# First cross-attention of a four-layer kernel: context times projection weights made once, probabilities divided ahead of their transposition, tile loop written out

## The chip, the cores and the metric

The kernel runs on one core of a Trainium2 chip. The metric is the device time of one execution in microseconds, as the median of several. The program computes four transformer layers (a cross-attention and a feed-forward part each); the change touches the first cross-attention alone, a stretch of about 70 us near the start.

## The reference, cut to what matters

`c` is the layer-normalised input (2 batches of 1024 tokens of 256), `q` the context (2 batches of 64 tokens of 256). `W_l` has 4 blocks of 256 columns, one for each part of the concatenation.

```python
def _L0_xattn_ref(c, q, w_cq, b_cq, w_c, b_c, w_q, b_q, W_l, b_l):
    cq = jnp.einsum('bcd,bqd,d->bcq', c, q, w_cq) + b_cq
    s = (c @ w_c + b_c)[:, :, None] + (q @ w_q + b_q)[:, None, :] + cq
    a = jax.nn.softmax(s, axis=2)
    c2q_att = jnp.einsum('bcq,bqd->bcd', a, q)
    b_att = jax.nn.softmax(jnp.max(s, axis=2), axis=1)
    q2c_att = jnp.einsum('bc,bcd->bd', b_att, c)[:, None, :]
    x = jnp.concatenate([c, c2q_att, c * c2q_att, c * q2c_att], axis=-1)
    return x @ W_l.T + b_l
x = x + _L0_xattn_ref(_layernorm(x), ctx_1024, ...)
```

The stretch computes blocks two and three: u = a q, and u W2 + (c*u) W3. Blocks one and four need sums over all tokens and are made behind it.

## The kernel before, in words

The 2048 tokens are 16 tiles of 128; one turn of the loop takes the tiles `it` of both batches together, so there are 8 turns, called turn 0 to turn 7 below. The arguments of `step` are four tiles in a row: `step(one, two, three, four)` finishes tile `one`, while `two`, `three` and `four` are in earlier phases. `first` runs the early phases of tiles 0, 1 and 2 before turn 0. The order on each engine is the order in which the functions are called in `first` and `step`; engines meet through semaphores (`wait_ge` and `then_inc`), and nothing reorders.

The way of one tile: VectorE normalises it (`normal`, L682) - TensorE transposes it (`transposes`, L560) - ScalarE copies it to `cT` (L635) - TensorE makes scores: a bias (L566) and the product with the scaled context (L570) - VectorE takes row maxima (L688) - ScalarE takes the exponential into `a` and its sums (L641) - TensorE transposes `a` (L577), ScalarE copies it to `aT` (L648) - TensorE multiplies with the context (`mix`, L584) - VectorE divides by the sums and multiplies with c: `uv` (L695, L700, L703) - TensorE transposes `uv`, 8 blocks (L592), ScalarE copies them to `uvT` (L654) - TensorE projects with 8 products of 256 columns (`project`, L602) - VectorE adds to the residual `x_res` (L709). A float32 product that is no transposition stands in the trace as two matmuls, a transposition as one. GpSimd keeps copies of c and cT and adds the bias of the projection (L735 to L739).

The loop is made by `pipeline`: turns 0 to 4 are one hardware loop, turns 5, 6 and 7 stand behind it as loops of one turn each, without the calls whose tile is past the end. TensorE's order in a turn: `probs_transposed(two)`, `scores(three)`, `mix_transposed(one)`, `transposes(four)`, `mix(two)`, `project(one)`. VectorE's: `maxima(three)`, `normal(four)`, `mixed(two)`, `add(one)`.

Of the kernel before, what the change touches and what calls it, by code (L numbers as in the profile page):

```python
# [7 lines left out]
ALU = mybir.AluOpType  # L8
# [471 lines left out]
def l0_xattn(e, given, ffn):  # L480
# [3 lines left out]
    with ExitStack() as ctx:  # L484
# [11 lines left out]
        aT = sb("aT", [P, P])  # L496
        uv = sb("uv", [P, 2, 2, D])
        uvT = sb("uvT", [P, 2, 4, P])
# [11 lines left out]
        with nc.Block(no_gpsimd_drain=True) as block:  # L510
# [15 lines left out]
            def _(v):  # L526
# [13 lines left out]
                s.mix_ready, s.out_psum, s.x_done, s.bias_added)  # L540
        each = (s.probs_ready, s.mix_psum, s.mixT_psum, s.mixT_ready)
        begin(1, *both)
        begin(2, *each)
        C_BANK, SCORES, MIX, MIX_T, OUT, PROBS_T = 0, 1, 2, 4, 6, 7
        pair_of = lambda buf, it: buf.rearrange("p (b t) n -> p b t n", b=BATCH)[:, :, bass.ds(it, 1), :].rearrange("p b t n -> p b (t n)")
        with nc.Block(no_gpsimd_drain=True) as block:
# [7 lines left out]
            def _(pe):  # L554
# [19 lines left out]
                def probs_transposed(it):  # L574
                    pe.wait_ge(s.probs_ready.sem, s.probs_ready.at(it, 2))
                    pe.wait_ge(s.probsT_ready.sem, s.probsT_ready.before(it))
                    pe.transpose(ps[PROBS_T][:, 0:P], flat(a[:]), e.ident[:]).then_inc(s.probsT_psum.sem, 1)  # L577

                def mix(it):
                    pe.wait_ge(s.probsT_ready.sem, s.probsT_ready.at(it))  # L580
                    pe.wait_ge(s.mix_ready.sem, s.mix_ready.before(it))
                    for b in range(BATCH):
                        own = slice(b * CTX, (b + 1) * CTX)
                        pe.matmul(ps[MIX + b][:, 0:D], aT[own, :], e.ctx_tok[own, b, :], start=True, stop=True)\  # L584
                          .then_inc(s.mix_psum.sem, 1)

                def mix_transposed(it):
                    pe.wait_ge(s.mix_ready.sem, s.mix_ready.at(it))
                    for b in range(BATCH):
                        pe.wait_ge(s.mixT_ready.sem, s.mixT_ready.before(it, b + 1))  # L590
# [3 lines left out]
                        mm.then_inc(s.mixT_psum.sem, 1)  # L594

                def project(it):
                    pe.wait_ge(s.x_done.sem, s.x_done.before(it))
                    for b in range(BATCH):
                        pe.wait_ge(s.mixT_ready.sem, s.mixT_ready.at(it, b + 1))
                        own = slice(b * D, (b + 1) * D)  # L600
                        for k in range(4):
                            mm = pe.matmul(ps[OUT][:, own], uvT[:, b, k, :], w_l[:, 2 + k, :], start=(b, k) == (0, 0), stop=k == 3,  # L602
                                           skip_group_check=True)
                    mm.then_inc(s.out_psum.sem, 1)

                def first(one, two, three):
# [20 lines left out]
                turns_of_tiles(pe, e.chain["pe"], first, step, depth=4)  # L627

            @block.scalar
            def _(act_):  # L630
# [14 lines left out]
                def copy_aT(it):  # L645
                    act_.wait_ge(s.probsT_psum.sem, s.probsT_psum.at(it))
                    act_.wait_ge(s.mix_psum.sem, s.mix_psum.before(it, 2))
                    nc.scalar.copy(aT[:], ps[PROBS_T][:, 0:P]).then_inc(s.probsT_ready.sem, 1)  # L648

                def copy_uvT(it):  # L650
                    act_.wait_ge(s.out_psum.sem, s.out_psum.before(it))
                    for b in range(BATCH):
                        act_.wait_ge(s.mixT_psum.sem, s.mixT_psum.at(it, b + 1))
                        nc.scalar.copy(flat(uvT[:, b, :, :]), ps[MIX_T + b][:, :]).then_inc(s.mixT_ready.sem, 1)  # L654

                def first(one, two, three):
# [5 lines left out]
                    exp(two)  # L662

                def step(one, two, three, four):
                    if two is not None:
                        copy_aT(two)
                    copy_uvT(one)
# [5 lines left out]
                turns_of_tiles(act_, act, first, step, depth=4)  # L673

            @block.vector
            def _(v):
# [14 lines left out]

                def mixed(it):
                    v.wait_ge(s.probs_ready.sem, s.probs_ready.at(it, 2))
                    for b in range(BATCH):
# [2769 lines left out]
```

## Time and profile before

| | us |
|---|---|
| median of 3 runs | 1603.34 (1602.52 to 1605.77) |
| the profiled execution, its own time | 1602.76 |
| its span, first to last instruction | 1601.0 |
| first cross-attention's loop, first transposition to last addition | 22.5 to 90.6 |
| mean granted TensorE clock | 0.925 |

The span is the time between the first and the last instruction in the profile; 1.8 us of the execution's time lie outside it. In rows of the timeline the columns are: start in us from the span's beginning, length in us, engine, source line, operation, output<-inputs, count of instructions merged, and in brackets the idle time of the engine just before and what ended it. PEld is TensorE's weight load. The length of a merged matmul row ends with the modelled end of the last one, which overlaps the next row: the pace of TensorE is read from starts, not from lengths.

### The profile page before, as it was taken

The page shows a single profiled execution, that of the slowest core. Times are in us where ns is not written, and L with a number is a line of the kernel's source. Part 1 is how long each engine was busy: PE and PEld are TensorE (multiplying, and loading weights), DVE is VectorE, ACT ScalarE, POOL GpSimd, SP SyncE. Part 2 cuts the span into 40 slices and gives each one's busy share as a digit, 9 for nine tenths or more (in the row PEclk, how much of TensorE's full clock was granted, in tenths as well). Part 3 has the DMA queues.
Part 4 walks back from the last instruction along what each step waited for, and adds up shares of the span by engine and source line. Part 5 has one row for each costly group of instructions (what it writes and reads, how often), then busy time and mean ns, then how long its engine had stood idle before and what let it go on. Part 6 is the DMA issues. An engine that isn't in the chain of part 4 may idle for free. (4 is left out here: it accounts for less than half of the span.)

```text
span 1601.0 us, 29168 instructions
## 1 busy us (share of the span) xinstructions
PE 1356.9 (85%) x9286; PEld 1066.1 (67%) x9287; DVE 1019.5 (64%) x2724; ACT 763.4 (48%) x1822; POOL 536.6 (34%) x584
## 2 busy tenths in 40 slices
PE   4977999999999999999998797919945689739993
PEld 3855877877787778877876465716733357539993
DVE  3446776767677777777774754358968769662223
ACT  1323665556655665666565234126746456313331
POOL 3222222222222323232321206545642624225551
PEclk9988999999999999999999798959977589969997
DMA  8000000000000100000001444244010000102124
GB/s 312 21 1 1 1 1 1 0 1 0 0 27 2 36 1 0 0 0 0 0 1 34 182 197 142 89 154 172 1 41 1 3 4 2 53 24 68 65 66 168
DMA packets 29278, 74.94 MB, mean 47 GB/s; under 512 B 7800, under 2 KB 13193, under 8 KB 27389
## 3 DMA queue, kind: packets, MB, share of 16 engines
q1 hardware_dynamic: 22364, 55.63, 9.3%
q0 software_dynamic: 6816, 18.14, 3.6%
q8 instruction: 46, 0.75, 0.2%
q14 instruction: 52, 0.42, 0.1%
HBM read 54.41 MB, written 20.88 MB: 47 GB/s over the span
## 5 line engine op out<-in xcount | busy, mean ns | idle before, releaser
L1107 PE MATMUL banks<-l_ffn_in_wqkv,l_ffn_hT 128*128 128x512 f32 x384 | 178.3, 600 | 0.0
L1190 PE MATMUL banks<-l_ffn_h2T,l_ffn_in_w 128*128 128x128 f32 x1408 | 175.7, 277 | 0.0
L1190 PEld LDWEIGHTS banks<-l_ffn_h2T,l_ffn_in_w 128*128 128x128 f32 x1408 | 167.0, 192 | 7.3 <-issue 5.7
L1319 ACT ACTIVATE l_ffn_work<-l_ffn_work,l_ffn_att_bias 128x256 f32<-128x256 f32 x256 | 126.4, 495 | 70.6 <-DVE l_ffn_att_bias L1475 70.6
L1348 ACT ACTIVATE l_ffn_gate<-banks,l_ffn_layer_cols 128x128 f32<-128x128 f32 x160 | 51.7, 364 | 183.5 <-PE banks L1190 170.2
L1041 POOL TENSOR_TENSOR l_ffn_rden_wide<-l_ffn_att_rden,ones 128x512 f32<-128x512 f32 x32 | 33.2, 1039 | 251.0 <-DVE l_ffn_att_rden L1486 251.0
L1107 PEld LDWEIGHTS banks<-l_ffn_in_wqkv,l_ffn_hT 128*128 128x128 f32 x384 | 68.1, 190 | 71.7 <-issue 71.6
L1198 PE MATMUL banks<-l_ffn_in_w,l_ffn_ff 128*128 128x256 f32 (+1 forms) x384 | 104.5, 388 | 0.0
L2981 POOL TENSOR_TENSOR L__probs<-L__probs,L__rec 128x1024 f32<-128x1024 f32 x32 | 60.9, 1902 | 100.5 <-DVE L__rec L2941 100.5
L1046 POOL TENSOR_TENSOR l_ffn_rstd<-l_ffn_ve,neg_half 128x1 f32<-128x1 f32 x32 | 20.0, 625 | 208.6 <-DVE l_ffn_ve L1512 208.6
L1356 ACT ACT_TABLE_LOAD x68 | 87.2, 1283 | 1.2
L2435 PEld LDWEIGHTS banks<-l_experts_rowT,l_plan_c_all 128*128 128x128 f32 x624 | 77.5, 196 | 1.9
L2435 PE MATMUL banks<-l_experts_rowT,l_plan_c_all 128*128 128x128 f32 x624 | 77.6, 279 | 0.0
L1130 PE MATMUL banks<-l_ffn_in_kT,l_ffn_qT 64*128 64x256 f32 x512 | 75.4, 392 | 2.3 <-ACT l_ffn_qT L1313 2.3
L1031 POOL TENSOR_TENSOR l_ffn_rn<-l_ffn_ss,neg_half 128x8 f32<-128x8 f32 x32 | 52.6, 1643 | 70.6 <-DVE l_ffn_ss L1427 70.6
L1139 PEld LDWEIGHTS banks<-ident,l_ffn_work 128*128 128x128 f32 x512 | 57.4, 141 | 27.7 <-issue 14.8
L1528 DVE SCALAR_TENSOR_TENSOR l_ffn_ff<-banks,l_ffn_layer_cols,l_ffn_gate 128x128 f32<-128x128 f32 x192 | 58.1, 344 | 26.1 <-ACT l_ffn_gate L1348 21.3
L2444 PE MATMUL banks<-l_ffn_in_w,l_experts_upT 128*128 x312 | 73.6, 379 | 0.0
L1198 PEld LDWEIGHTS banks<-l_ffn_in_w,l_ffn_ff 128*128 128x128 f32 (+1 forms) x384 | 63.0, 190 | 14.5 <-issue 10.6
L1139 PE MATMUL banks<-ident,l_ffn_work 128*128 128x128 f32 x512 | 64.5, 275 | 6.8 <-ACT l_ffn_work L1319 6.8
L1481 DVE COPY l_ffn_pT<-banks 128x512 f32<-128x512 f32 x64 | 42.6, 666 | 35.1 <-PE banks L1139 35.1
L1155 PE MATMUL banks<-l_ffn_pT,l_ffn_in_vv 128*64 128x128 f32 x1024 | 63.0, 276 | 0.0
(444 smaller groups left out, 3348.7 us busy)
## 6 DMA issues: line engine op xcount, KB each, us to landing
l_plan_rows<-l_plan_pairs SPq DMA_DIRECT2D x16, 512.0 KB, 8.0
l_ffn_in_w<-in_L_w SPq DMA_DIRECT2D x2, 4096.0 KB, 17.5
l_ffn_in_down<-in_L_down SPq DMA_DIRECT2D x1, 4096.0 KB, 13.6
l_plan_pairs<-l_plan_rows SPq DMA_DIRECT2D x4, 1024.0 KB, 7.0
l_plan_table<-l_plan_rows SPq DMA_DIRECT2D x8, 512.0 KB, 2.7
l_ffn_in_wqkv<-in_L_wqkv SPq DMA_DIRECT2D x1, 3072.0 KB, 12.0
l_ffn_in_w<-in_L_w SPq DMA_DIRECT2D x4, 640.0 KB, 12.3
x_res<-in_x SPq DMA_DIRECT2D x4, 512.0 KB, 5.3
```

The lines of the kernel that those rows point to most:

```text
L1107: mm = pe.matmul(ps[:, (Q, K, V)[n], :], hT[:, m.b, m.odd, ch, 1 - ch:P + 1 - ch], wqkv[:, bass.ds(m.layer, 1), ch, n * INNER:(n + 1) * IN ...
L1130: mm = pe.matmul(ps[:, SCORES + 2 * g + n, half * 2 * P:(half + 1) * 2 * P], qT[own, m.b, j, :], flat(kT[own, m.b, j, :, :]), start=True, ...
L1139: mm = pe.transpose(ps[:, SCORES + j, n * P:(n + 1) * P], work[:, m.b, 2 * j + n // 2, (n % 2) * P:(n % 2 + 1) * P], e.ident[:])
L1155: mm = pe.matmul(ps[n * DH:(n + 1) * DH, MIXED, j * P:(j + 1) * P], vv[:, m.b, c, h * DH:(h + 1) * DH], pT[:, m.b, 2 * slot_of(h) + c, :], ...
L1190: mm = pe.matmul(ps[:, HIDDEN[pair], to:to + P], w1[:, ch, at:at + P], h2T[:, ch, m.b, :], start=(j % 2, n, ch) == (0, 0, 0), stop=ch == D ...
L1198: mm = pe.matmul(ps[:, DOWN, 0:D], ff[units(j), j, :], w2[units(j), bass.ds(m.layer, 1), j, :].rearrange("p l n -> p (l n)"), start=j == 0 ...
L1319: ex = nc.scalar.activation(work[:, m.b, slot, :], work[:, m.b, slot, :], ACT.Exp, bias=bias[:, m.b, slot:slot + 1], scale=-1.0, accum_out ...
L1356: act.link(nc.scalar.activation(unused[:], zero, func))
L1528: ins = v.scalar_tensor_tensor(ff[own, j, :], ps[own, HIDDEN[pair], of:of + P], cols[own, col:col + 1], gate[own, j, :], ALU.add, ALU.mult)
L2435: mm = pe.matmul(ps[m.j][:, f * P:(f + 1) * P], up_w[:, m.j, at:at + P], rowT[:, m.j, ch, :], start=(f, ch) == (0, 0), stop=ch == DCH - 1, ...
L2444: mm = pe.matmul(ps[3 + m.j][:, 0:D], upT[:, m.j, f, :], down_weight(x, f), start=f == 0, stop=f == MCH - 1)
L2981: p.tensor_tensor(probs[:, m.b, :, :], probs[:, m.b, :, :], rec[:, m.b, :].unsqueeze(2).broadcast_to((P, XH, CTX)), ALU.mult)\
```

## The change

The projection of u is folded: u W2 = a (q W2). `ctx_w` = q W2 is made once (`folded`, four matmuls in the trace) and copied by ScalarE. Per tile, `project` takes `aT` times `ctx_w` (64 rows of the array for each batch) and only c*u goes the long way, over 4 transpositions instead of 8 and 4 products instead of 8. So that `a` is divided before it is transposed, VectorE does `divide` (a reciprocal and a product of 128x128) between the exponential and the transposition of `a`; `mixed` is then one product that reads PSUM. `aT` has two buffers, since the projection reads it a turn later. The output of the projection takes two PSUM banks, the transposed product one. The loops of TensorE, ScalarE and VectorE are written out in Python; GpSimd's remains. TensorE's order in a turn has `scores(three)` ahead of `probs_transposed(two)`; VectorE's begins with `divide(two)`.

```diff
@@ TensorE
 def probs_transposed(it):
-    pe.wait_ge(s.probs_ready.sem, s.probs_ready.at(it, 2))
+    pe.wait_ge(s.scaled.sem, s.scaled.at(it))
+def folded():
+    for ch in range(DCH):
+        mm = pe.matmul(ps[MIX_T][:, 0:D], e.ctxT[:, ch, :, :], w_l[:, 2 + ch, :], start=ch == 0, stop=ch == DCH - 1)
+    mm.then_inc(s.kT_ready.sem, 1)
 def mix_transposed(it):
     for b in range(BATCH):
-        for k in range(4):
-            mm = pe.transpose(ps[MIX_T + b][:, k * P:(k + 1) * P],
-                              uv[:, b, k // 2, (k % 2) * P:(k % 2 + 1) * P], e.ident[:])
+        for ch in range(DCH):
+            k = b * DCH + ch
+            mm = pe.transpose(ps[MIX_T][:, k * P:(k + 1) * P], cu[:, b, ch * P:(ch + 1) * P], e.ident[:])
 def project(it):
     pe.wait_ge(s.x_done.sem, s.x_done.before(it))
     for b in range(BATCH):
-        own = slice(b * D, (b + 1) * D)
-        for k in range(4):
-            mm = pe.matmul(ps[OUT][:, own], uvT[:, b, k, :], w_l[:, 2 + k, :], start=(b, k) == (0, 0), stop=k == 3,
+        own = slice(b * CTX, (b + 1) * CTX)
+        pe.matmul(ps[OUT + b][:, 0:D], aT[own, it % 2, :], ctx_w[own, :], start=True, stop=False)
+    pe.wait_ge(s.mixT_ready.sem, s.mixT_ready.at(it))
+    for b in range(BATCH):
+        for ch in range(DCH):
+            mm = pe.matmul(ps[OUT + b][:, 0:D], cuT[:, b * DCH + ch, :], w_l[:, 4 + ch, :], start=False, stop=ch == DCH - 1)
 def first(one, two, three):
     ...
     mix(one)
+    folded()
+    pe.wait_ge(s.kT_ready.sem, s.kT_ready.at(0, 2))
 def step(one, two, three, four):
+    if three is not None:
+        scores(three)
     if two is not None:
         probs_transposed(two)
-    if three is not None:
-        scores(three)
@@ ScalarE
 def copy_aT(it):
-    act_.wait_ge(s.mix_psum.sem, s.mix_psum.before(it, 2))
+    if it >= 2:
+        act_.wait_ge(s.out_psum.sem, s.out_psum.at(it - 2))
+def copy_ctx_w():
+    act_.wait_ge(s.kT_ready.sem, s.kT_ready.at(0))
+    nc.scalar.copy(ctx_w[:], ps[MIX_T][:, 0:D]).then_inc(s.kT_ready.sem, 1)
@@ VectorE
+def divide(it):
+    v.wait_ge(s.probs_ready.sem, s.probs_ready.at(it, 2))
+    dve.link(v.reciprocal(a_rec..., a_sum...[:, :, it:it + 1]))
+    v.tensor_tensor(a[:], a[:], a_rec[:].unsqueeze(2).broadcast_to((P, BATCH, CTX)), ALU.mult).then_inc(s.scaled.sem, 1)
 def mixed(it):
-    (two reciprocals, two products u = PSUM * a_rec, one product of both batches with c)
+    v.tensor_tensor(cu[:], e.psum[:, MIX:MIX + BATCH, 0:D], pair_of(c_all[:], it)..., ALU.mult).then_inc(s.mix_ready.sem, 1)
 def first(one, two, three):
     normal(one)
     normal(two)
     maxima(one)
+    divide(one)
     normal(three)
     maxima(two)
     mixed(one)
 def step(one, two, three, four):
+    if two is not None:
+        divide(two)
     if three is not None:
         maxima(three)
```

The order on TensorE in turn 5 before (turns 0 to 4 have besides the transpositions L560 x4 ahead of L584). L577 is the transposition of `a`, L566 and L570 the scores, L592 the transpositions of `uv`, L584 the mix, L602 the projection:

```order
L577 MATMUL banks<-ident,l_xattn_a 128x128
L566 MATMUL banks<-l_xattn_q_bias,ones 128x128
L570 MATMUL banks<-l_xattn_qcat,cT 128x64 x4
L592 MATMUL banks<-ident,l_xattn_uv 128x128 x8
L584 MATMUL banks<-ctx_tok,l_xattn_aT 128x256 x2
L602 MATMUL banks<-l_xattn_in_w_l,l_xattn_uvT 128x256 x8
```

And TensorE in a turn of the change that still has all its calls (turns 0 to 4):

```order
L576 MATMUL banks<-l_xattn_q_bias,ones 128x128
L580 MATMUL banks<-l_xattn_qcat,cT 128x64 x4
L587 MATMUL banks<-ident,l_xattn_a 128x128
L608 MATMUL banks<-ident,l_xattn_cu 128x128 x4
L570 MATMUL banks<-ident,c_tile 128x128 x4
L599 MATMUL banks<-ctx_tok,l_xattn_aT 128x256 x2
L615 MATMUL banks<-l_xattn_ctx_w,l_xattn_aT 128x256 x2
L619 MATMUL banks<-l_xattn_in_w_l,l_xattn_cuT 128x256 x4
```

The scores moved ahead of the transposition of `a`; four transpositions and four whole products went, two half-height products came, right behind the two of the mix.

VectorE in turn 5 before (maxima, reciprocals, u, c*u, addition):

```order
L688 TENSOR_REDUCE l_xattn_nmax<-banks 128x2
L695 RECIPROCAL l_xattn_a_rec<-l_xattn_a_sum 128x1 x2
L700 TENSOR_SCALAR l_xattn_uv<-banks,l_xattn_a_rec 128x256 x2
L703 TENSOR_TENSOR l_xattn_uv<-l_xattn_uv,l_xattn_c_all 128x2x256
L709 TENSOR_TENSOR x_res<-banks,x_res 128x2x256
```

And of the change:

```order
L717 RECIPROCAL l_xattn_a_rec<-l_xattn_a_sum 128x2
L718 TENSOR_TENSOR l_xattn_a<-l_xattn_a,l_xattn_a_rec 128x128
L711 TENSOR_REDUCE l_xattn_nmax<-banks 128x2
L724 TENSOR_TENSOR l_xattn_cu<-banks,l_xattn_c_all 128x512
L731 TENSOR_TENSOR x_res<-banks,x_res 128x2x256
```

The reciprocal went ahead of the maxima with a product behind it, right after the addition of the turn before; of the three products between maxima and addition one is left.

## Rows read from the trace of the kernel before

**Rows 1.** Windows: busy time of each engine, granted clock (PEclk), DMA share, GB/s.
```profile
22.00:26.00 4.00, 2.83 (x12) 2.43 (x13) 2.02 (x4) 1.02 (x2) 3.05 (x5) 1.00 1.05 428
28.80:32.20 3.40, 3.39 (x17) 3.06 (x17) 0.42 (x3) 0.27 (x1) 1.89 (x3) 1.00 0.93 393
50.86:58.27 7.41, 6.99 (x44) 5.79 (x43) 3.42 (x9) 2.53 (x8) 2.39 (x3) 1.00 0.00 0
118.00:120.00 2.00, 1.29 (x6) 0.78 (x5) 1.97 (x4) 1.95 (x4) 0.37 (x1) 1.00 0.00 0
```

**Rows 2.** Timeline of turn 3 with the start of turn 4, all engines.
```profile
58.27 0.27 PE L577 MATMUL banks<-ident,l_xattn_a 128*128 128x128 f32 x1
58.58 0.69 DVE L709 TENSOR_TENSOR x_res<-banks,x_res 128x512 f32 x1 [1.97 <-PE banks L602]
58.60 1.00 PE L570 MATMUL banks<-l_xattn_qcat,cT 128*128 128x64 f32 x8
58.67 0.27 ACT L648 COPY l_xattn_aT<-banks 128x128 f32<-128x128 f32 x1 [3.17 <-PE banks L577]
59.44 1.04 PE L592 MATMUL banks<-ident,l_xattn_uv 128*128 128x128 f32 x8
59.75 0.29 DVE L688 TENSOR_REDUCE l_xattn_nmax<-banks 128x128 f32 x1 [0.48 <-PE banks L570]
60.11 0.74 DVE L682 TENSOR_SCALAR c_tile<-x_res,mean_var,rstd 128x256 f32 x2
60.91 0.66 PE L560 MATMUL banks<-ident,c_tile 128*128 128x128 f32 x4 [0.42 <-DVE c_tile L682]
61.49 0.70 PE L584 MATMUL banks<-ctx_tok,l_xattn_aT 64*128 64x256 f32 x4
62.12 3.72 PE L602 MATMUL banks<-l_xattn_in_w_l,l_xattn_uvT 128*128 128x256 f32 x16
65.47 0.14 PEld L577 LDWEIGHTS banks<-ident,l_xattn_a 128*128 128x128 f32 x1
65.68 0.27 PE L577 MATMUL banks<-ident,l_xattn_a 128*128 128x128 f32 x1
```

**Rows 3.** Timeline of the last turns, 5 to 7.
```profile
73.09 0.27 PE L577 MATMUL banks<-ident,l_xattn_a 128*128 128x128 f32 x1
79.53 0.27 PE L577 MATMUL banks<-ident,l_xattn_a 128*128 128x128 f32 x1
84.80 1.04 PE L592 MATMUL banks<-ident,l_xattn_uv 128*128 128x128 f32 x8
86.22 3.69 PE L602 MATMUL banks<-l_xattn_in_w_l,l_xattn_uvT 128*128 128x256 f32 x16 [0.39 <-ACT l_xattn_uvT L654]
```

**Rows 4.** Timeline of `first` and of turn 0.
```profile
28.81 0.47 PE L577 MATMUL banks<-ident,l_xattn_a 128*128 128x128 f32 x1 [1.28 <-ACT l_xattn_a L641]
33.52 0.47 PE L577 MATMUL banks<-ident,l_xattn_a 128*128 128x128 f32 x1 [0.20 <-ACT l_xattn_a L641]
34.32 1.81 PE L570 MATMUL banks<-l_xattn_qcat,cT 128*128 128x64 f32 x8
37.63 1.06 PE L560 MATMUL banks<-ident,c_tile 128*128 128x128 f32 x4
38.62 1.23 PE L584 MATMUL banks<-ctx_tok,l_xattn_aT 64*128 64x256 f32 x4
39.78 3.83 PE L602 MATMUL banks<-l_xattn_in_w_l,l_xattn_uvT 128*128 128x256 f32 x16
```

**Rows 5.** Groups by line, shapes kept apart, VectorE.
```profile
L2029 DVE TENSOR_TENSOR l_route_equal<-l_route_equal,l_route_expert_number 128x128 f32<-128x128 f32 x4 | 1.2, 292 | 0.1
L695 DVE RECIPROCAL l_xattn_a_rec<-l_xattn_a_sum 128x1 f32 x10 | 1.1, 151 | 0.0
L703 DVE TENSOR_TENSOR l_xattn_uv<-l_xattn_uv,l_xattn_c_all 128x512 f32<-128x512 f32 x8 | 5.5, 692 | 1.3 <-DVE l_xattn_uv L700 1.1
```

**Rows 6.** Waits from 20 to 92 us (total, times, longest); one timeline row of ScalarE.
```profile
DVE l_xattn_uv L703 <- DVE l_xattn_uv L700: 1.1, 5, 0.2
109.22 0.37 ACT L1296 COPY l_ffn_hT<-banks 128x256 f32<-128x256 f32 x1
```

More of the change, by code:

```diff
@@ L495, in l0_xattn @@
         a_rec = sb("a_rec", [P, 2])
-        aT = sb("aT", [P, P])
-        uv = sb("uv", [P, 2, 2, D])
-        uvT = sb("uvT", [P, 2, 4, P])
+        aT = sb("aT", [P, 2, P])
+        ctx_w = sb("ctx_w", [P, D])
+        cu = sb("cu", [P, BATCH, D])
+        cuT = sb("cuT", [P, BATCH * DCH, P])
         top = sb("top", [P, BATCH])
@@ L539, in l0_xattn, with unrolled @@
         both = (s.c_kept, s.cT_kept, s.c_ready, s.cT_psum, s.cT_ready, s.scores_psum, s.max_ready, s.probsT_psum, s.probsT_ready,
-                s.mix_ready, s.out_psum, s.x_done, s.bias_added)
-        each = (s.probs_ready, s.mix_psum, s.mixT_psum, s.mixT_ready)
+                s.mix_ready, s.out_psum, s.x_done, s.bias_added, s.mixT_psum, s.mixT_ready, s.scaled)
+        each = (s.probs_ready, s.mix_psum)
+        begin(2, s.kT_ready)
         begin(1, *both)
         begin(2, *each)
-        C_BANK, SCORES, MIX, MIX_T, OUT, PROBS_T = 0, 1, 2, 4, 6, 7
+        C_BANK, SCORES, MIX, MIX_T, OUT, PROBS_T = 0, 1, 2, 4, 5, 7
+        def unrolled(engine, order, first, step):
+            order.begin(engine)
+            each_tile = [*range(TILES), None, None, None]
+            first(*each_tile[0:3])
+            for n in range(TILES):
+                step(*each_tile[n:n + 4])
         pair_of = lambda buf, it: buf.rearrange("p (b t) n -> p b t n", b=BATCH)[:, :, bass.ds(it, 1), :].rearrange("p b t n -> p b (t n)")
@@ L583, in mix @@
                         own = slice(b * CTX, (b + 1) * CTX)
-                        pe.matmul(ps[MIX + b][:, 0:D], aT[own, :], e.ctx_tok[own, b, :], start=True, stop=True)\
+                        pe.matmul(ps[MIX + b][:, 0:D], aT[own, it % 2, :], e.ctx_tok[own, b, :], start=True, stop=True)\
                           .then_inc(s.mix_psum.sem, 1)
@@ L625, in step @@
                     project(one)
-                turns_of_tiles(pe, e.chain["pe"], first, step, depth=4)
+                unrolled(pe, e.chain["pe"], first, step)
             @block.scalar
@@ L662, in first @@
                     exp(two)
+                    copy_ctx_w()
                 def step(one, two, three, four):
@@ L666, in step @@
                         copy_aT(two)
-                    copy_uvT(one)
+                    copy_cuT(one)
                     if four is not None:
@@ L671, in step @@
                         exp(three)
-                turns_of_tiles(act_, act, first, step, depth=4)
+                unrolled(act_, act, first, step)
             @block.vector
@@ L727, in step @@
                     add(one)
-                turns_of_tiles(v, dve, first, step, depth=4)
+                unrolled(v, dve, first, step)
             @block.gpsimd
@@ L740, in l0_xattn @@
         end(TILES, *both, *each)
+        end(1, s.kT_ready)
         s.max_ready.each(2)
```

32 lines of the change are left out of this document (12 added, 20 removed).

## The prediction

> **What bounds the kernel now.** I read the windows first, then the timeline. TensorE is busy 6.99 of the 7.41 us of turn 2, VectorE 3.42 and ScalarE 2.53 [rows 1]: in a steady turn TensorE has the work, and what it waits for is VectorE. The timeline of turn 3 [rows 2] shows how, counted from its first matmul at 58.27. The transposition of `a` and the scores run until 1.17, the 8 transpositions of `uv` (L592) from 1.17 to about 2.1; then 0.42 us of idle (0.65 by its weight loads) until the normalised tile is there at 2.64 (60.91), because VectorE may take the maxima (1.48) only after the scores and normalises behind that. Transpositions and the mix take to 3.85 (62.12), the projection 3.56 to 7.41 (65.68). So the projection is almost half of the turn, and each of its 16 matmuls is worth about 0.21 us (the weight loads run from 62.12 to 65.47, 3.35 us for 16). Turn 5 takes 6.44, turn 6 5.27, turn 7 4.98 us up to the end of its projection (86.22 + 16 x 0.222 = 89.78) [rows 3]. In `first` and the early part of turn 0 TensorE is at half its later pace: 4 transpositions and what follows take 0.99 us at 37.63 and 0.58 at 60.91, the mix 1.16 at 38.62 and 0.63 at 61.49; from 39.78 on the pace is the later one (16 matmuls in 3.67) [rows 2, 4]. That is the lower clock level, 1.2 GHz, until about 40 us and 2.4 GHz behind it, though the column of the granted clock reads 1.00 in both [rows 1].
>
> **The steady turns (1 to 4), part by part.** Again from the first matmul behind the last projection.
> - VectorE: the addition starts at 0.31 and ends at 1.00 as now [rows 2]. Then comes `divide`: a reciprocal of 0.15 and a product of 128x128 in SBUF, 0.29 (L2029, same shape, also with a broadcast operand) [rows 5]. With 0.03 between instructions it ends at 1.50. Between an instruction and one that waits for it the trace has more in one place: 1.1 us in 5 waits ahead of L703, 0.22 each [rows 6]; that would give 1.70. I take 1.50, since L703 waits for a reader of PSUM and the reciprocal reads SBUF.
> - TensorE: scores from 0 to 1.06 (moved ahead, they hide two thirds of the wait for `divide`), idle until 1.55, `a` transposed, 4 transpositions of `cu` to 2.1. Maxima 1.53 to 1.82 and the normalised tile at 2.61: transpositions at 2.68 against 2.64 now. So the 4 transpositions saved (0.44) buy nothing: they turn into the idle time ahead of L587. Mix at 3.27.
> - Projection: four half-height matmuls behind the four of the mix. Four halves now take 0.63 from 61.49 to 62.12 [rows 2] where four whole ones take 0.85; two groups are 1.26 at most, and 1.07 if the pairs follow without a break (4 x 0.2135 + 0.2). I take 1.26. Then 8 whole matmuls, 1.71. End 6.24 against 7.41: **1.17 us a turn, 4.7 for four turns**. Bounds: 1.17 - 0.20 (the longer link) = 0.97, and 1.17 + 0.19 = 1.36.
> - Hidden: `copy_aT` (1.95 to 2.22), `copy_cuT` (2.4 to 3.0, one copy instead of two), `mixed` (one product of 0.69 [rows 5], from about 4.0) end before TensorE asks for them. Behind `divide` on VectorE wait the maxima, the next tile and `mixed`; their delay is the 0.04 above. GpSimd needs 2.39 us a turn [rows 1]. Should `copy_cuT` come late its price is at most the 0.6 that it takes.
>
> The Trainium skill, "TensorEngine Tiling (Array Packing)", section Theoretical Speedup, promises up to twice the rate for a contraction of at most 64 rows. The rows show 0.63 for four halves where that rule says 0.43. By the rule the eight halves would be 0.85 instead of 1.26 and the whole sum 0.4 x 7 = 3 us larger; I go by the row.
>
> Against the change speaks the Trainium skill, "VectorE: DVE Perf Modes", section on the TRN2 errata: a fixed latency is exposed by every instruction, so that small ones cost mostly that. The product of 128x128 at 0.292 against 0.692 for four times the elements [rows 5] agrees. Its formula of 58 cycles plus one per element gives 0.19, and 0.1 us a turn less; the trace's 0.29 stands.
>
> **The last turns.** Turn 5 has no next tile. `a` transposed at 1.55, its copy done 2.22 (ScalarE starts 0.40 behind the matmul, 58.67 - 58.27 [rows 2], and takes 0.27), mix and halves 2.27 to 3.53, 1.71 more: 5.24 against 6.44, gain 1.2. Turn 6 has no scores, so nothing covers `divide` any more: again 5.24, against 5.27, gain 0. Turn 7: 4 transpositions, the halves wait for the addition (1.06), 0.63, 1.71: 3.40 against 4.98, gain 1.6. **Together 2.8**, so 7.5 us with the steady ones.
>
> **The front.** `divide(0)` puts the first transposition of `a` 0.54 later (28.81 [rows 4]: recip, product, hand-over), and nothing covers it, as everything behind it waits. `folded` adds 4 matmuls of 256 columns at the low level, 0.43 each, twice the 0.2135: 1.7. Then TensorE waits for ScalarE's copy of `ctx_w`: hand-over 0.4, copy of 256 columns 0.37 [rows 6], 0.75 in all. The wait for the exponential (0.20) goes. So turn 0 begins at 36.3 instead of 33.52. Up to its transpositions 4.11 us pass now (37.63); then the scores 2.13 (twice 1.06) and the chain of maxima, normalisation and hand-overs, 1.47 from the scores' end (59.44 to 60.91 [rows 2]), 3.60: transpositions at 39.9 against 37.63, 2.3 late. What remains of turn 0 is 5.82 us now (to 43.45: the projection's start 39.78 and 3.67). In the change it is 0.59 + 1.26 + 1.71 = 3.56 at the high level and twice, about 6.8, at the low one. With the rise at 40 us as before turn 0 ends at 43.5, no change; with all of it low at 46.7, 3.2 late. I take 0.5 late, near the first: TensorE is nearly as dense from 29 to 40 us as now, where it is busy 3.39 of 3.40 [rows 1]. **Front: +0.5 (-1.2 to +3.2).** The lower bound is a rise some 3 us earlier, by the dense matmuls of `folded`.
>
> **The loop written out** I cost at nothing: behind the taken branch at the end of turn 3 the next weight load starts at 65.47, right where the last one of the projection ends (62.12 + 3.35), and the short pauses ahead of the mix and the projection double in turn 0 [rows 2, 4], so they follow the array's clock, not register arithmetic. If the branches did hide something on another engine, it is under TensorE's work.
>
> **Sum.** -7.5 + 0.5 = -7.0 against the profiled execution's own 1602.76 (span 1601.0 and 1.8 around it): 1595.8. The median of the runs shown is 0.6 above that execution, so I expect 1596.4. Everything behind the stretch only shifts.
>
> **The rivals.**
> - *The clock rises a turn's length later and the links cost 0.2.* -7.5 + 6 x 0.2 + 3.2 = -3.1: 1602.8 - 3.1 + 0.6 = 1600.3. For it: the front has three new pauses (0.54, 0.75, 0.3 us), and now it takes until 40 us for TensorE to get the high level after a start with holes (busy 2.83 of 4 us at 22) [rows 1]. Against: these pauses are short beside those at 22 to 29.
> - *More gain:* the halves follow at full overlap (7 x 0.19 = 1.3) and the clock rises early (1.7 more): 1596.4 - 3.0 = 1593.4. For it: `folded` is 1.7 us of unbroken whole matmuls.
> - *Slower: the level stays low through the stretch.* A steady turn then is 2 x (1.06 + 0.11 + 0.44 + 0.59 + 1.26 + 1.71) = 10.3 us of TensorE work, against 7.41: +2.9 in each of four, +2.7, +1.8 and +0.6 in turns 5 to 7, +3.2 in turn 0: +20, 1623. It decides once the rise is 20 us late: each turn at the low level costs 10.3 - 6.24 = 4.1, and two of them eat the gain. For it: TensorE's idle share in a turn rises from 6% to 17%. Against: at the low level it would have no idle time at all, and a stretch with TensorE busy 1.29 of 2 us keeps the high level now [rows 1].
> - *The change does not shorten the path:* if VectorE were the engine that bounds the turn. Its 3.42 us of 7.41 fall (two products of 256 columns go, one of 128 comes); it is a partner in the chain, not the bound. Price at most 0.44 a turn (the halves of L592, already given up), so this has no case of its own.
>
> **How the numbers follow.** Forecast 0.60 (own range 1594.5 to 1599), late clock 0.17, more gain 0.12, slower by the clock 0.04, something behind the stretch that shifts with it 0.07, half of it to either side. 0.2% (3.2 us) is about what a measurement of this kernel tells from no change; faster is below 1600.1: 0.60 + 0.12 + a quarter of the late clock + 0.02 = 0.77; within 0.15; slower 0.08. The range 1593.5 to 1601.5 leaves out the slow case and the outer part of the early clock.
>
> **What would show it.** In the changed profile: four steady turns of 6.0 to 6.4 us between matmuls of L576; an idle of about 0.5 ahead of L587, released by VectorE's L718; transpositions L570 released by the normalised tile; 1.1 to 1.3 us from L599 to L619; turn 7 of about 3.4; a pause of about 0.75 ahead of the third scores; the double pace of the mix and projection from 40 to 43 us. Wrong would make it: turns of over 7 us, matmuls of turn 1 at the low pace, or another length of what follows the last addition.

## The result, and the profile after

The changed kernel took 1591.69 us (median of 6 runs, 1589.65 to 1593.3), the kernel before 1602.59 (6 runs, 1598.47 to 1605.77): ratio 0.9929 [0.9915, 0.9943], 10.9 us less. The forecast was 1596.4 with a range from 1593.5. The direction was right and the gain half as large again as forecast, so that the time lies below the range. The profiled execution took 1591.43 (span 1589.6) against 1602.76 (1601.0).

Windows of the changed kernel: core, columns and the first two stretches as in [rows 1], the third one is its turn 2.

```profile
22.00:26.00 4.00, 3.21 (x14) 2.81 (x15) 1.64 (x3) 0.95 (x2) 3.42 (x5) 1.00 1.05 392
28.80:32.20 3.40, 3.24 (x15) 2.96 (x15) 1.05 (x4) 0.27 (x1) 1.84 (x2) 1.00 0.92 393
47.36:53.09 5.73, 5.47 (x36) 4.35 (x35) 2.65 (x7) 2.04 (x7) 2.39 (x3) 1.00 0.01 1
```

A turn takes 5.73 us where it took 7.41, and TensorE is busy 5.47 of it where it was busy 6.99: of the 1.68 us that went, 1.52 are work that it no longer has and 0.16 idle time. The timeline of turn 2 of the changed kernel (start, duration, engine, line, idle time before and its releaser) answers to [rows 2]:

```profile
47.36 0.39 PE L576 MATMUL banks<-l_xattn_q_bias,ones 128*128 128x128 f32 x2
47.56 0.69 DVE L731 TENSOR_TENSOR x_res<-banks,x_res 128x512 f32<-128x512 f32 x1 [1.57 <-PE banks L619]
48.17 0.16 DVE L717 RECIPROCAL l_xattn_a_rec<-l_xattn_a_sum 128x2 f32<-128x2 f32 x1
48.36 0.29 DVE L718 TENSOR_TENSOR l_xattn_a<-l_xattn_a,l_xattn_a_rec 128x128 f32<-128x128 f32 x1
48.62 0.29 DVE L711 TENSOR_REDUCE l_xattn_nmax<-banks 128x2 f32<-128x128 f32 x1
48.70 0.14 PEld L587 LDWEIGHTS banks<-ident,l_xattn_a 128*128 128x128 f32 x1 [0.26 <-DVE l_xattn_a L718]
48.71 0.33 PE L587 MATMUL banks<-ident,l_xattn_a 128*128 128x128 f32 x1
48.83 0.73 DVE L705 TENSOR_SCALAR c_tile<-x_res,mean_var,rstd 128x256 f32<-128x256 f32 x2
49.61 0.42 PEld L570 LDWEIGHTS banks<-ident,c_tile 128*128 128x128 f32 x4 [0.38 <-DVE c_tile L705]
50.20 0.70 PE L599 MATMUL banks<-ctx_tok,l_xattn_aT 64*128 64x256 f32 x4
50.73 0.60 PE L615 MATMUL banks<-l_xattn_ctx_w,l_xattn_aT 64*128 64x256 f32 x4
51.26 1.99 PE L619 MATMUL banks<-l_xattn_in_w_l,l_xattn_cuT 128*128 128x256 f32 x8
53.09 0.38 PE L576 MATMUL banks<-l_xattn_q_bias,ones 128*128 128x128 f32 x2
```

From L576 on: `a` is transposed 1.35 later (forecast 1.55), `c` 2.25 (2.68), the mix comes at 2.84 (3.27), the mix and the halves take 1.06 (1.26), the whole products 1.83 (1.71). Ahead of its weight loads TensorE idles 0.26 us for `divide` and 0.38 for the normalised tile; before, it idled 0.65 for the tile alone:

```profile
60.90 0.42 PEld L560 LDWEIGHTS banks<-ident,c_tile 128*128 128x128 f32 x4 [0.65 <-DVE c_tile L682]
```

On VectorE the addition starts 0.20 behind the turn's first matmul, 0.31 before, and the normalisation 0.21 behind the start of the maxima, 0.36 before [rows 2]: a first hint at what the forecast left out.

The front of the changed kernel answers to [rows 4]:

```profile
28.96 0.48 PE L587 MATMUL banks<-ident,l_xattn_a 128*128 128x128 f32 x1 [1.80 <-DVE l_xattn_a L718]
33.41 1.92 PE L591 MATMUL banks<-l_xattn_in_w_l,ctxT 128*128 128x256 f32 x4
35.78 0.49 PE L576 MATMUL banks<-l_xattn_q_bias,ones 128*128 128x128 f32 x2 [0.46 <-ACT l_xattn_ctx_w L671]
36.11 1.00 PE L580 MATMUL banks<-l_xattn_qcat,cT 128*128 128x64 f32 x8
39.80 1.99 PE L619 MATMUL banks<-l_xattn_in_w_l,l_xattn_cuT 128*128 128x256 f32 x8
```

The eight scores at 36.11 take 1.00, the same eight before took 1.81 at 34.32 [rows 4]: TensorE is at its higher level, 2.4 GHz, from about 35 us instead of 40. The column of the granted clock shows 1.00 on both sides of the rise, so the durations have to be read.

The last turns answer to [rows 3]. Turn 6 waits for `divide` (1.19), turn 7 for the addition (0.35):

```profile
70.84 0.33 PE L587 MATMUL banks<-ident,l_xattn_a 128*128 128x128 f32 x1 [1.19 <-DVE l_xattn_a L718]
75.38 0.70 PE L615 MATMUL banks<-l_xattn_ctx_w,l_xattn_aT 64*128 64x256 f32 x4 [0.35 <-DVE x_res L731]
78.05 0.69 DVE L731 TENSOR_TENSOR x_res<-banks,x_res 128x512 f32<-128x512 f32 x1 [2.72 <-PE banks L619]
```

A clean measure of the stretch is the start of VectorE's last addition of each turn (turn 0, turn 1, ..., turn 7, us; before L709, after L731), read from each kernel's timeline:

| kernel | 0 | 4 | 5 | 6 | 7 | steady turn |
|---|---|---|---|---|---|---|
| before | 43.76 | 73.40 | 79.73 | 85.00 | 89.95 | 7.41 |
| changed | 41.83 | 64.76 | 69.70 | 74.64 | 78.05 | 5.73 |

The last addition is 11.90 us earlier, of which the span keeps 11.4. By part: turn 0 ends 1.93 earlier, turns 1 to 4 give 6.71, turn 5 gives 1.39, turn 6 0.33, turn 7 1.54.

### The profile page after: what moved, and what is told of

Read it like the earlier page. It is cut to its first block and busy times, and to the rows that moved or that the text cites. A ratio compares the mean times of both kernels' runs of the same rounds, so it can differ in the third digit from the quotient of the medians.

```text
span 1589.6 us, 28758 instructions
## 1 busy us (share of the span) xinstructions
PE 1345.3 (85%) x9226; PEld 1054.7 (66%) x9227; DVE 1013.2 (64%) x2708; ACT 758.7 (48%) x1815; POOL 534.3 (34%) x584
## 2 busy tenths in 40 slices
DMA packets 29278, 74.96 MB, mean 47 GB/s; under 512 B 7799, under 2 KB 13192, under 8 KB 27388
```

## The experiments

Three groups of runs, each beside runs of the kernel before: group 1 is the first four kernels, group 2 the next four, group 3 the last four. The kernel before took 1591.43 in group 1 (17 runs), 1601.88 in group 2 (11), 1603.14 in group 3 (23); in group 1 the times are some 11 us shorter, in the profiles of its four kernels in a later part with the experts' DMA transfers (102 us against 112 to 114 from the first row of the routing, `l_route_equal`, to the first addition of the experts' rows to `x_res`). So only ratios, and stretches within a profile, are compared across groups. Additions are given as in the table above.

**The loops of the kernel before, written out.** The arithmetic stays that of the kernel before.

```diff
-turns_of_tiles(v, dve, first, step, depth=4)        # and the same for pe and act_
+unrolled(v, dve, first, step)
```

> The kernel before with the three loops of TensorE, ScalarE and VectorE written out and nothing else. Theory A (the writing out takes register instructions off VectorE's part of the chain): the first normalised tile 0.3 to 0.5 us earlier, and 0.15 us between the maxima and the normalisation in each of turns 0 to 4, so a steady turn of 7.25 instead of 7.41; in all -1.2 us, about 1601.4 against 1602.6, ratio 0.999. Theory B (my prediction's: it costs and brings nothing): turn 7.41, ratio 1.000. Theory C (the loops hid most of what I missed): -3 us or more, turn 7.1 or less. The clock's rise should stay near 40 us under A and B, since TensorE's work is the same.

Additions 42.72 (turn 0), 71.28, 77.62, 82.89, 87.84: a steady turn takes 7.14 instead of 7.41, the last addition is 2.11 earlier. The four steady turns give 1.08 of that; the other 1.04 is turn 0, in whose front the first tile came 0.5 earlier (21.20) and the clock rose at about 38.5 us instead of 40. Three rows of VectorE in it, maxima, normalisation and addition:

```profile
57.00 0.69 DVE L717 TENSOR_TENSOR x_res<-banks,x_res 128x512 f32<-128x512 f32 x1 [1.92 <-PE banks L610]
58.17 0.29 DVE L696 TENSOR_REDUCE l_xattn_nmax<-banks 128x2 f32<-128x128 f32 x1 [0.48 <-PE banks L578]
58.38 0.73 DVE L690 TENSOR_SCALAR c_tile<-x_res,mean_var,rstd 128x256 f32<-128x256 f32 x2
```

From maxima to normalisation it is 0.21, as in the changed kernel. But the whole kernel is slower: 1597.19, ratio 1.0051 [1.0034, 1.0067]. From the start of the last addition to the first row of the routing (`l_route_equal`, at 940.7) it takes 852.9 us where it took 846.5, in the kernel before (936.5 - 89.95) and in the changed one (924.6 - 78.05). The loss is outside the stretch; the two experiments below that repeat and pad this kernel find most of it.

**The change with VectorE's loop as a hardware loop again.** All else is the change.

```diff
-unrolled(v, dve, first, step)
+turns_of_tiles(v, dve, first, step, depth=4)
```

> The changed kernel with VectorE's loop as a hardware loop again (TensorE and ScalarE stay written out). Theory A: the steady turn gets longer by 0.15 to 0.35 (5.9 to 6.1 instead of 5.73), the start 0.4 later: +1.2 to +2.2 us, 1593 to 1594. Theory B (VectorE's shorter hand-overs come from the changed order and not from the loop): turn 5.73, no change. The clock rises at the same place in the work.

1583.41, ratio 0.9961 [0.9948, 0.9974]. Additions 45.75, 69.75, 74.68, 79.62, 83.03: a steady turn of 5.99, 0.26 more than the change. The first normalised tile comes at 21.69 instead of 21.19. VectorE in a steady turn whose first matmul starts at 51.47:

```profile
51.78 0.69 DVE L731 TENSOR_TENSOR x_res<-banks,x_res 128x512 f32 x1 [1.47 <-PE banks L619]
52.84 0.29 DVE L711 TENSOR_REDUCE l_xattn_nmax<-banks 128x128 f32 x1
53.19 0.74 DVE L705 TENSOR_SCALAR c_tile<-x_res,mean_var,rstd 128x256 f32 x2
```

0.35 again from the maxima to the normalisation, and 0.31 from the matmul to the addition: 0.14 and 0.11 more than in the change (0.21 and 0.20), which together is the 0.26 of the turn, to a hundredth. Taken off the kernel before, with the other two, and put back on the changed one, VectorE's loop is worth 0.26 to 0.27 us a steady turn. TensorE's and ScalarE's loops, which stay written out here, bring nothing more that shows. The first tile is 0.5 later in both kernels with the loop, but also in a written-out one (21.77, the padded kernel below), so the 0.5 cannot be put down to the loop alone.

**The folded product made in the block before.** `folded` and its copy leave the path between turns.

```diff
 @@ block that makes kT, TensorE
+for ch in range(DCH): mm = pe.matmul(ps[4][:, 0:D], e.ctxT[:, ch, :, :], w_l[:, 2 + ch, :], ...)
 @@ first
-folded()
-pe.wait_ge(s.kT_ready.sem, s.kT_ready.at(0, 2))
```

> The changed kernel with the product of context and weights and its copy made in the block before the loop, so that TensorE's sequence in the front has neither the four matmuls nor the pause behind them. Theory D (the whole matmuls of the product bring the clock's rise forward from 40 to 35 us): without them in the loop's front the rise comes at 38 us or later, turn 0 is run at the low level, and the 2.4 us saved there are given back: between -0.5 and +1.5 us. Rival E (the rise comes at about 35 us whatever stands there, or by chance of its phase): -1.0 to -2.4 us, 1589.5 to 1590.7, with the transpositions of turn 0 already at the high level.

1580.32, ratio 0.9944 [0.993, 0.9957]. The third scores start at 34.41 instead of 35.78, though the first normalised tile comes 1.67 later (22.86 instead of 21.19; the copy of `ctx_w` and the products stand ahead of it). But TensorE reached the higher level only at about 39.1, and the additions (42.16, 65.09, 70.03, 74.96, 78.37) are not earlier than the change's. A gain of 1.4 was hidden by a clock that rose 4 us later.

**The normalisation of the tile four turns on, ahead of the addition.**

```diff
-if four is not None: normal(four)     # between maxima and mixed
 if two is not None: mixed(two)
+if one + 4 < TILES: normal(one + 4)
 add(one)
```

> The changed kernel with the normalisation of the next tile moved ahead of the addition, one turn earlier, so that it is done under the projection. Theory F (a steady turn is set by the chain addition, divide, maxima, normalisation, transposition): the transpositions of the next tile no longer wait, 0.35 us less in each of turns 0 to 4, turn 5.4: -1.7 us, 1590. Rival G (TensorE's own work or ScalarE's copies set the turn): no change, 5.7.

1578.72, ratio 0.993 [0.991, 0.995]. Additions 41.28, 63.35, 68.29, 73.23, 76.64: a steady turn of 5.52, and the last addition 1.41 ahead of the change's. TensorE's rows:

```profile
42.58 0.33 PE L587 MATMUL banks<-ident,l_xattn_a 128*128 128x128 f32 x1 [0.27 <-DVE l_xattn_a L718]
43.18 0.60 PE L570 MATMUL banks<-ident,c_tile 128*128 128x128 f32 x4
46.60 0.38 PE L576 MATMUL banks<-l_xattn_q_bias,ones 128*128 128x128 f32 x2
```

The wait ahead of L570 is gone; the one for `divide` is all that is left in a turn. In the time of the whole kernel the 1.41 us do not show: the ratio, 0.993, is that of the change (0.9929), and behind the last addition this profile takes 848.7 us up to the routing instead of 846.5.

**The change a second time**, unaltered, for what the clock does by itself.

> The changed kernel once more, unaltered, timed beside the kernel before on one chip, with a second profile. What it tells apart: whether the rise of TensorE's clock in the front, at about 35.1 us in the first profile of the change and at 40.0 in that of the kernel before, belongs to the kernel or to the execution. Theory H (chance of the execution: the written-out, the half-written-out and the folded-ahead variants rose at 38.5, 43.3 and 39.1): another moment than 35, anywhere from 35 to 43, turn 0 then ends between 41.8 and 45, everything from turn 1 on shifts by that. Rival D (the whole matmuls of the folded product bring it): 35 to 36 again. The time against before on one chip: stage 11.9 us shorter in the profile, 10 to 12 with the clock's chance, ratio 0.992 to 0.994.

1592.44, ratio 0.994 [0.9924, 0.9957]; its profiled execution took 1598.88. Its front:

```profile
33.43 2.07 PE L591 MATMUL banks<-l_xattn_in_w_l,ctxT 128*128 128x256 f32 x4
36.55 1.81 PE L580 MATMUL banks<-l_xattn_qcat,cT 128*128 128x64 f32 x8
42.44 2.16 PE L619 MATMUL banks<-l_xattn_in_w_l,l_xattn_cuT 128*128 128x256 f32 x8
```

The same eight scores take 1.81 instead of 1.00; the higher level comes at about 42.5, 7 us later than in the first profile of the same kernel. Turn 0 ends with the addition at 44.64 instead of 41.83; all later turns are equal to 0.01 (5.73; last addition 80.86). So 2.8 us between the two profiles are the moment of the rise alone. The last addition is 9.1 ahead of the 89.95 before in this profile and 11.9 in the first; neither of the two rose at the 40 us of the kernel before, where the gain would lie in between (an estimate: a rise 2.5 us earlier than in the second profile spares half of that, 1.25, so about 10.3). Another 4.7 of the 7.5 us between the two profiles lie behind the stretch: 851.2 us from the last addition to the routing against 846.5, of the same program. Counted by ScalarE's table loads, 2.5 of them fall in the first 77 us behind the last addition and 1.4 in the last 66 ahead of the routing; I have no cause for them. This profiled execution was also the slowest of its six, whose median is 1592.44. `folded` stood at the same place in both, so its dense matmuls do not by themselves bring an early rise. In the six profiles that have `folded` there, the halved durations of TensorE's rows begin at 35 to 36 us in three and at 42.5 to 44 in three; in the eight without it they begin between 37 and 40.

**Both edits together**: the folded product in the block before, and the normalisation ahead.

> The changed kernel with both: the folded product in the block before the loop, and the normalisation of the next tile ahead of the addition. If their effects add: turns of 5.52 and the front 2.4 us shorter less 1.3 for the longer block before, that is 2.3 us less than the change at the same moment of the clock's rise, 1.0 to 4 us with its chance; ratio to before 0.990 to 0.993. If the clock's rise gives the front's part back: 1.0.

1589.93 (7 runs), ratio 0.9923 [0.9907, 0.9938]: the lowest ratio here, 2.5 us under the change in the same group, but the intervals overlap, so that it is faster than the change is not shown. A steady turn takes 5.52 again; the last addition is at 78.11 with a rise at about 40, against 80.86 with 42.5.

**Old order on TensorE**, the scores behind the transposition of `a`.

```diff
-if three is not None: scores(three)
 if two is not None: probs_transposed(two)
+if three is not None: scores(three)
```

> The changed kernel with the order of before in one place: the transposition of the divided probabilities ahead of the next tile's scores. Theory (the move of the scores is what hides the division): TensorE idles about 1.3 us at the start of each steady turn, the scores come after it, and maxima and normalisation behind them; the transpositions of the next tile 3.7 us into the turn instead of 2.25: turn 7.1 instead of 5.73, about +7 us over turns 0 to 4, so nearly all the steady gain gone. Rival (the chain on VectorE is short enough to be hidden anyhow): turn below 6.2.

1603.39 (one run), additions 45.29, 74.32, 80.33, 85.27, 88.68: a turn of 7.26. TensorE in it:

```profile
53.69 0.33 PE L587 MATMUL banks<-ident,l_xattn_a 128*128 128x128 f32 x1 [1.18 <-DVE l_xattn_a L718]
56.12 0.66 PE L570 MATMUL banks<-ident,c_tile 128*128 128x128 f32 x4 [0.59 <-DVE c_tile L705]
```

`divide` uncovered is 1.18 of idle time, and the maxima and the normalisation behind the scores come late too: 1.53 us a turn, nearly all of the change's gain. With `divide` in the chain, the gain hangs on the order of two calls.

**The half-height products apart**, one batch after the other.

```diff
+pe.wait_ge(s.mixT_ready.sem, s.mixT_ready.at(it))
 for b in range(BATCH):
     pe.matmul(ps[OUT + b][:, 0:D], aT[own, it % 2, :], ctx_w[own, :], start=True, stop=False)
-pe.wait_ge(s.mixT_ready.sem, s.mixT_ready.at(it))
-for b in range(BATCH):
     for ch in range(DCH): ...
```

> The changed kernel with the same eight half-height matmuls of mix and projection, but those of the projection no longer in a row: batch 0's half product, its whole ones, batch 1's half product, its whole ones. Theory (the halves are cheap because pairs on different rows of the array run at the same time, 0.27 us a pair in a row): from the first mix matmul to the next turn 3.2 to 3.35 us instead of 2.90, turn 6.0 to 6.2. Rival (a half-height matmul is cheap by itself): 2.90, turn 5.73.

1598.23 (one run), a turn of 6.55, 0.82 more than the change:

```profile
45.45 0.70 PE L599 MATMUL banks<-ctx_tok,l_xattn_aT 64*128 64x256 f32 x4
45.98 0.59 PE L616 MATMUL banks<-l_xattn_ctx_w,l_xattn_aT 64*128 64x256 f32 x2
46.51 1.13 PE L618 MATMUL banks<-l_xattn_in_w_l,l_xattn_cuT 128*128 128x256 f32 x4
47.57 0.70 PE L616 MATMUL banks<-l_xattn_ctx_w,l_xattn_aT 64*128 64x256 f32 x2
48.19 1.13 PE L618 MATMUL banks<-l_xattn_in_w_l,l_xattn_cuT 128*128 128x256 f32 x4
49.16 0.38 PE L576 MATMUL banks<-l_xattn_q_bias,ones 128*128 128x128 f32 x2
```

From the mix to the next turn 3.71 us pass, in the change 2.90. A pair of records of L616 takes 0.53 and 0.62 here, where four take 0.53 in the change: alone, a half-height product costs more than a whole one of the change, where eight records take 1.83, a pair 0.46. The whole products between them take 0.20 more as well. In turns 5 to 7, where the halves now also wait for the copy of `cu` (0.19, 0.19 and 0.82 us), the loss is 1.24 to 1.27.

**The written-out kernel before, again**, unaltered.

> The kernel before with its three loops written out, once more. Its first profile was 2.1 us shorter in the stretch itself (turn 7.14 instead of 7.41, first tile 0.5 earlier), but 6 us longer in the feed-forward loop behind it, where VectorE waited 5.2 us ahead of one line (the scale of the attention, twice, about 100 us apart) instead of 3.0 without waiting for anything that the profile shows, and TensorE's clock fell to the low level twice behind it. Theory I (the written-out code moves VectorE's later loop to other places of its instruction stream, and instructions come late there): the same again, 5 us waits, ratio 1.003 to 1.006. Rival (chance of the execution): waits of 3.0 us, ratio about 0.9985.

1608.37 (12 runs), ratio 1.004 [1.0024, 1.0056]; the turn is 7.14 again, and from the last addition to the routing 855.1. In the first feed-forward part VectorE stands ahead of the same instruction, with nothing that the profile shows to wait for. The row of the kernel before, then of the first written-out run, then of this one:

```profile
251.00 0.28 DVE L1460 TENSOR_SCALAR l_ffn_att_scale<-l_ffn_rn 128x2 f32<-128x2 f32 x2 [2.91 <-issue]
```

```profile
248.55 0.29 DVE L1468 TENSOR_SCALAR l_ffn_att_scale<-l_ffn_rn 128x2 f32<-128x2 f32 x2 [5.18 <-issue]
```

```profile
250.29 0.29 DVE L1468 TENSOR_SCALAR l_ffn_att_scale<-l_ffn_rn 128x2 f32<-128x2 f32 x2 [5.11 <-issue]
```

And the windows of this run around it (columns as in [rows 1]):

```profile
250.00:255.00 5.00, 2.42 (x10) 1.89 (x11) 4.33 (x22) 3.57 (x15) 0.00 (x0) 0.71 0.01 2
255.00:260.00 5.00, 5.00 (x18) 2.77 (x18) 4.07 (x7) 2.75 (x6) 1.67 (x2) 0.61 0.00 0
```

TensorE runs dry behind that pause, and the granted clock falls to 0.71 and 0.61, where it is 1.00 in the kernel before. What the pauses cost can be read from the starts of ScalarE's table loads (`ACT_TABLE_LOAD`), of which the feed-forward loop has the same ones in every kernel. Between two of them, in us, in an undisturbed turn 13.3; "padded" is the next experiment:

| from (start in the kernel before) | before | written out | written out, again | padded |
|---|---|---|---|---|
| 244.24 | 15.5 | 19.4 | 19.4 | 13.3 |
| 336.66 | 15.7 | 18.9 | 19.0 | 13.3 |
| 611.33 | 14.4 | 14.4 | 14.4 | 16.9 |
| 702.59 | 14.4 | 14.4 | 14.4 | 18.2 |

The first two rows hold the pauses: about 3.0 us in the kernel before and 5.0 to 5.2 in the written-out one. They are 7.2 us of the loss, the same in both runs. The last 66 us ahead of the routing add 1.5 to 1.7, and the first 77 behind the last addition took 2.6 us less in the first run and 0.1 less in this one. Over all profiles the piece from the last addition to the routing takes 851.8 to 856.9 us in the four kernels with the old projection written out, and 845.8 to 851.2 in the ten others, the unaltered change with both 846.5 and 851.2 among them. So one profile's sum says little about it; the 7.2 us at two places in both runs, the means, 854.2 and 847.9, and the ratios of 12 and 6 runs say that the loss goes with this code. The changed kernel, written out as well, has pauses of 3.1 and 2.8 us there, like the kernel before; nothing in the edit was meant to bring that, so it is luck.

**The same, with 24 small instructions more on VectorE** ahead of the stretch, to move all later code of VectorE.

```diff
+for n in range(24):
+    v.memset(uv[:, 1, 1, n:n + 1], 0.0)
```

> The same with 24 instructions more on VectorE (memsets of one column each) in the block before, where VectorE waits for a load and they are hidden; they only shift where its later code lies. Theory I: the waits of 5.2 us change, to 3.0 as in the kernel before or to another length, and the time with them: 1 to 6 us less than the unpadded one, ratio 0.997 to 1.002. Rival (the place of the code does not matter): as the unpadded one within 1 us, waits 5.2.

The pause moved: 0.40 instead of 5.1 at this place, and 3.15 and 3.11 came up at the same line at 616 and 710 us, where no other kernel has one of over 2 us; ahead of one row of `oT` it is 5.5, as in two variants of the change, 3.3 in the kernel before. The time did not move: 1609.89 (12 runs), ratio 1.0036 [1.0022, 1.005], 856.9 us from the last addition to the routing.

```profile
250.12 0.28 DVE L1470 TENSOR_SCALAR l_ffn_att_scale<-l_ffn_rn 128x2 f32<-128x2 f32 x2 [0.40 <-issue]
```

So these pauses depend on where the code lies. Without padding they are the bulk of the loss (7.2 us by the table above); with it, compared with the kernel before, 4.6 us are gained at these two places and 6.3 lost at the two later ones, and the 5.5 ahead of `oT` costs 1.7. The padded kernel also takes 3.4 us more in the first 77 us and 3.1 more in the last 66. Why the place of the code makes VectorE pause is not shown, and neither is what makes up the rest. The first normalised tile comes at 21.77 here, as late as in the kernel before (21.70), though all three loops are written out.

**The division moved, no fold**: loops written out, `divide` and the scores as in the change, the projection as before.

```diff
+divide(two)      # and scores(three) ahead of probs_transposed(two)
-u = v.tensor_scalar(uv[:, b, 0, :], ps[MIX + b][:, 0:D], a_rec[:, b:b + 1], None, ALU.mult)
+u = v.tensor_copy(uv[:, b, 0, :], ps[MIX + b][:, 0:D])
```

> The kernel before with loops written out, the division ahead of the transposition and the scores ahead of it, but without the folded product: 8 transpositions and 8 whole products as before (u is copied out of PSUM undivided). Theory (the gain of a steady turn comes from the projection, the move of the division neither costs nor gains as long as the scores hide it): turn 7.1 to 7.25, against 7.14 without the division's move. Rival (the shorter chain on VectorE behind the mix is what gains): turn below 6.9.

1608.19 (one run), additions 43.17, 71.59, 78.26, 84.92, 89.87. The steady turn is 7.10 against 7.14 without the division: moved and covered, it is free in the steady turns. Turn 5, which has scores but no next tile, takes 6.67 instead of 6.34, and turn 6, without scores, 6.66 instead of 5.27: uncovered it costs 1.4. All of the gain of a steady turn beyond the loop is then the fold: 7.10 to 5.73.

**The kernel before, again.**

> The kernel before, unaltered, a second profile. Theory H (the moment of the clock's rise is the execution's chance): steady turns of 7.41 and the same waits on VectorE (3.0 in the feed-forward part), but turn 0 ends anywhere between 41 and 46 us instead of 43.45. Rival: 43.4 to 43.5 again.

1598.58 (one run); turn 7.41, additions 43.53, 73.17, 79.50, 84.77, 89.72, rise at about 39.9. Here the clock rose where it did in the first profile, 40.0. That it can vary by 7 us, as in the changed kernel, was not seen in these two; the two profiles of the written-out kernel before differ by about 1.5 (rise at 38.5 and 37, turn 0's addition at 42.72 and 41.99).

## Why the prediction fell short, step by step

- **Steady turns** (forecast 1.17 each, measured 1.68). The mechanism was right: the fold takes work off TensorE, the scores cover `divide`, the four transpositions saved (0.44) turn for the most part into idle time. By its weight loads TensorE idles 0.65 us in a turn before and 0.90 in the change with VectorE's loop put back; in the change itself it is 0.64, as the loop's part is gone. Of the 0.51 that was missing, 0.43 lies ahead of the mix (2.84 instead of 3.27): 0.25 of it is the loop, as with VectorE's loop put back the mix comes at 3.09, and 0.18 is the chain of `divide`, maxima and normalisation, which I took too long. The halves are 0.20. The whole products take 0.12 of it back (1.83 instead of 1.71).
- **"The loop written out I cost at nothing": this step failed.** VectorE is a link of the turn's chain, and its own loop is worth 0.26 to 0.27 us of it, 1.1 us over four turns. It was shown both ways. The first tile also comes 0.5 earlier, but the padded kernel leaves open that this is the loop. I had looked for the loop's cost on TensorE, at the taken branch, and found none; on VectorE, [rows 2] has the normalisation 0.36 behind the maxima though these take 0.29, and the addition 0.31 behind the first matmul, and I read both as the usual distances. The step should have had bounds like the others.
- **Halves** (forecast 1.26 for eight with those of the mix, bounds 1.07 to 1.26; measured 1.06 to 1.07). I took the end without overlap. Over turns 0 to 6 this is 1.3 us. The halves apart show what overlap is worth: 0.82 a turn. The Trainium skill, "TensorEngine Tiling (Array Packing)", section Theoretical Speedup, promised up to twice the rate; 0.53 for the four halves of L615 against the 0.85 that [rows 2] give for four whole products is 1.6 times. That lies between the 0.63 of my row and the 0.43 of that rule.
- **Last turns** (forecast 1.2, 0 and 1.6; measured 1.39, 0.33 and 1.54). Turns 5 and 6 both take 4.94 where I had 5.24: 0.19 is the halves, the other 0.11 the addition, which starts 0.20 instead of 0.31 behind the first matmul. In turn 5 that 0.11 does not count as gain, as the kernel before has it too when its hardware loop is over (6.33 from addition to addition, 6.44 from matmul to matmul).
- **Front** (forecast +0.5, bounds -1.2 to +3.2; measured -1.93, and +0.88 in the second profile of the change). About 0.5 is the earlier first tile (21.19 instead of 21.70), of which some 0.4 reach TensorE (28.44 instead of 28.81 for the first transposition of `a` in the kernel that is written out and nothing else). The delays of `divide` and `folded` came about as worked out (third scores at 35.78, forecast 36.3). What carried the first profile out of the bounds was the clock, at 35 instead of 40 us.
- **Behind the stretch** I expected only a shift: 846.5 us from the last addition to the routing in both first profiles. In the second profile of the change it was 4.7 more, and in the written-out kernels with the old projection 5 to 10 more, mostly at VectorE's pauses. That the change itself does not pay this is luck. That risk had 0.07 in the forecast, and it is real.
- **Sum.** 2.43 (front) + 2.01 (steady turns) + 0.19 + 0.33 - 0.06 (last turns) = 4.90, the difference between the 7.0 of the forecast and the 11.9 of the last addition. The rival "more gain" had two of its sources, full overlap and an early clock, at 1593.4 with a chance of 0.12; the third, the loop, was in no case, so the range ended too high. By the second profile's clock the stretch gives 9.1, still 2 more than forecast: loop and halves, not the clock, are what the forecast missed for certain. By themselves these two, 1.1 and 1.3, would give 1594.0, still in the range; it takes the earlier front as well to end below it, and that is in part the chance of an execution: the second measurement's ratio, 0.994, would put the kernel at 1593.0, close to the range's end. The chances named for "faster" add up to 0.78, not 0.77. A late clock did occur in one execution, the one with the rise at 42.5; the low level through the stretch never did.

## What to carry to other kernels

Ask what a hardware loop costs on each engine of the chain, not on the busiest one: the distance between two of its instructions, compared with the duration of the first, shows it. Put half-height products next to each other in a run, and put covered work ahead of a new wait: each of these two orders was worth 0.8 to 1.5 us of a 5.7 us turn. Judge a gain near the start of a program by two profiles at least, and read stretches behind the clock's rise apart from those before it. Compare also the time behind the edited stretch: written-out loops made the old kernel's stretch 2 us shorter and the kernel slower.

## What the runs showed of the hardware

- The moment at which TensorE's clock rose from 1.2 to 2.4 GHz in the front differed between executions of one and the same program: about 35 and 42.5 us. In both TensorE worked from 29 us on with one pause of 0.46 us, ahead of the third scores. Over all kernels it lay between 35 and 44.
- Written out, VectorE starts the normalisation before the recorded end of the maxima (0.21 behind the start of 0.29); in a hardware loop it does not (0.35), and the addition too starts 0.11 later. The maxima start ahead of the recorded end of `divide`'s product (0.29) either way, 0.26 behind its start written out and 0.21 in the loop. That addresses from registers are the reason is argued, not shown.
- A half-height product between whole ones costs 0.53 to 0.62 us, in a run of halves 0.27.
- The longest pause of VectorE without a shown releaser at one line between 100 and 450 us was 3.0 us in the kernel before, 5.1 to 5.2 in the written-out one, and 0.4 with 24 instructions more ahead of it, while 3.1 to 3.2 came up at the same line at 616 and 710 us. A turn with such a pause took 15.5 to 15.7 us (pause 3.0) and 18.9 to 19.4 (pause 5.0 to 5.2), an undisturbed one 13.3.
- Behind the stretch one and the same program took 846.5 us in one execution and 851.2 in another, up to the same instruction: 2.5 of the 4.7 us in the first 77 us, 1.4 in the last 66. The cause was not followed.
